# Output bias by one-row matmuls, one VectorE operation for the residual sum, and a placing step moved by a slot

## The reference, cut to what matters

```python
x = x + layernorm(attn0(layernorm(x)))            # phase 0 of the kernel
f = layernorm(x)
for l in range(2):                                # phases 1 and 2
    f = f + _attn(_ln(f, ln1_w[l], ln1_b[l]), ...)   # y @ wo + bo
    h = _ln(f, ln2_w[l], ln2_b[l])
    f = f + moe(h, ...)       # l = 0: two experts per token; l = 1: two per batch
x = x + layernorm(f)
```

## Time and profile before

| | |
|---|---|
| median of 3 runs | 1260.97 us (1259.69 to 1270.06) |
| the profiled execution | 1260.14 us, of it 1258.4 us from the first to the last instruction |
| steps of phases 0 and 1 | to about 620 us |
| expert jobs of phase 1 | about 640 to 775 us |
| steps of phase 2 | about 800 to 1125 us |
| batch experts and end | to 1258 us |

### The profile page before, as it was taken

The page is one execution under the profiler, slowest core; times in us unless marked ns, Lnnn a source line. Parts: engine busy times, 40 slices in busy tenths (PEclk is TensorE's granted clock), DMA queues, the critical chain, the costliest instruction groups (busy, mean ns, idle before and its releaser), DMA issues. The chain is left out here.

```text
span 1258.4 us, 38248 instructions
## 1 busy us (share of the span) xinstructions
PE 1048.2 (83%) x10356; PEld 791.0 (63%) x10451; DVE 974.2 (77%) x2902; ACT 789.2 (63%) x1905; POOL 683.7 (54%) x1018
## 2 busy tenths in 40 slices
PE   1888999999899999998289995487888988959997
PEld 0555666666666666665189995255555655638996
DVE  3678999999998899898647654368899898865665
ACT  1566777777677777776068774266666666745554
POOL 3345565555556778776623333557676676422332
PEclk9999999999999999999589998599999999988999
DMA  5332111111211222111122222233221121100000
GB/s 146 93 99 78 52 46 39 43 51 53 54 52 44 59 66 66 50 57 45 50 63 67 68 71 65 69 113 108 60 66 47 55 65 38 53 1 9 17 21 21
DMA packets 118044, 72.96 MB, mean 58 GB/s; under 512 B 8384, under 2 KB 112960, under 8 KB 117952
## 3 DMA queue, kind: packets, MB, share of 16 engines
q1 hardware_dynamic: 99296, 53.11, 15.2%
q10 hardware_dynamic: 14560, 10.35, 2.9%
q0 software_dynamic: 4096, 8.40, 2.2%
HBM read 21.68 MB, written 11.60 MB: 26 GB/s over the span
## 5 line engine op out<-in xcount | busy, mean ns | idle before, releaser
L608 DVE TENSOR_REDUCE negm<-bank 128x2 f32<-128x512 f32 (+1 forms) x576 | 389.5, 680 | 79.7 <-PE bank L300 55.0
L496 ACT ACTIVATE prob<-bank 128x512 f32<-128x512 f32 x576 | 339.6, 595 | 128.6 <-PE bank L322 90.4
L889 POOL TENSOR_SCALAR_AFFINE_SELECT prob<-prob 128x512 f32<-128x512 f32 x384 | 248.3, 648 | 171.3 <-ACT prob L496 169.7
L341 PE MATMUL bank<-prob,vaug 128*32 128x256 f32 (+1 forms) x3072 | 167.9, 337 | 1.6 <-POOL prob L889 1.3
L1181 POOL COPY w_job<-w_s 128x512 f32 x104 | 67.7, 651 | 164.6 <-PE bank L1150 156.0
L308 PE MATMUL bank<-stack 126*128 126x256 bf16 x768 | 151.7, 279 | 0.0
L327 PE MATMUL bank<-stack 128*128 128x256 bf16 x768 | 150.6, 278 | 0.9 <-ACT prob L496 0.9
L1172 ACT ACTIVATE prob<-bank,b_job 128x128 f32<-128x128 f32 (+1 forms) x416 | 133.4, 398 | 24.7 <-PE bank L1150 11.8
L1161 PE MATMUL bank<-w_job,prob 128*128 128x128 f32 x1088 | 138.9, 276 | 0.1
L1161 PEld LDWEIGHTS bank<-w_job,prob 128*128 128x128 f32 x1088 | 132.2, 192 | 2.1 <-issue 0.5
L341 PEld LDWEIGHTS bank<-prob,vaug 128*32 128x32 f32 x3072 | 81.4, 110 | 77.7 <-issue 45.8
(11 more groups left out here) (180 smaller groups left out, 2073.0 us busy)
## 6 DMA issues: line engine op xcount, KB each, us to landing
stack<-parts SPq DMA_DIRECT2D x288, 128.0 KB
w_s<-e_w ACTq DMA_DIRECT2D x32, 256.0 KB, 3.0
oT<-x_routed SPq DMA_DIRECT2D x72, 64.0 KB, 1.8
y_routed<-oT SPq DMA_DIRECT2D x36, 128.0 KB, 1.9
stack<-mT SPq DMA_DIRECT2D x192, 4.0 KB
out<-x_all SPq DMA_DIRECT2D x16, 128.0 KB, 1.8
b_all<-e_b ACTq DMA_DIRECT2D x2, 512.0 KB, 8.5
x_routed<-hk,x_at POOLq DMA_INDIRECT x64, 2.3
```

Source lines behind the costliest of these rows:

```text
L341: m = nc.tensor.matmul(o, w, (prob0, prob1)[kb][:, g % 2, h], start=kb == 0, stop=kb == 1, skip_group_check=True)
L496: nc.scalar.activation(o, s, ACT.Exp, scale=SCALE).then_inc(exp_done, 1)
L608: nc.vector.tensor_reduce(o, s, AX.X, ALU.max, negate=True).then_inc(max_done, 1)
L889: nc.gpsimd.affine_select(out=t, in_=t, compare_op=ALU.is_ge, fill=0.0, base=0, pattern=[[0, HG], [1, P]], channel_multiplier=-1).then_inc ...
```

## The change

In phases 1 and 2, `pe_o3` leaves the accumulation open and adds, for each of the two token halves, a matmul of one contraction row: a row of ones (1 x 128) as weights, the bias row (1 x 128) as the moving operand. DVE then reads PSUM, adds `f_all` and writes `f_all` in one operation; it raises the semaphore by 2. The bias addition into `att` stays in phase 0. In phase 1 the placing pieces 3 and 4 move from slot 3 to slot 2, piece 5 from the end of slot 3 to its first part.

```diff
@@ pe_o3
                 m = nc.tensor.matmul(post_bank[:, qb * P:(qb + 1) * P], onT[:, i.par, qb * P:(qb + 1) * P],
-                                     wo_s[:, i.phase], start=True, stop=True)
+                                     wo_s[:, i.phase], start=True, stop=i.phase == 0)
+                if i.phase > 0:
+                    m = nc.tensor.matmul(post_bank[:, qb * P:(qb + 1) * P], ones[0:1], bo_s[0:1, i.phase],
+                                         start=False, stop=True)
@@ dve_residual
-            base = NRES * i.v
             dve.wait_ge(o3_ps, i.v + 1)
+            if i.phase > 0:
+                nc.vector.tensor_tensor(pair(f_all, i), post_bank[:, 0:T].rearrange("p (j d) -> p j d", j=2),
+                                        pair(f_all, i), ALU.add).then_inc(res, 2)
+                return
             nc.vector.tensor_tensor(att[:, i.par], post_bank[:, 0:T].rearrange("p (j d) -> p j d", j=2),
                                     bo_s[:, i.phase:i.phase + 1].to_broadcast([P, 2, P]),
                                     ALU.add).then_inc(res, 1)
-            if i.phase > 0:
-                dve.wait_ge(res, base + 1)
-                nc.vector.tensor_tensor(pair(f_all, i), pair(f_all, i), att[:, i.par], ALU.add).then_inc(res, 1)
@@ dve_slot
-                dve_place(first, 3)
+                dve_place(first, 5)
...
+            if k == 2 and placing:
+                dve_place(first, 3)
...
+            if k == 2 and placing:
+                dve_place(first, 4)
...
-            if k == 3 and placing:
-                dve_place(first, 4)
-            if k == 3 and placing:
-                dve_place(first, 5)
```

## The result

The changed kernel takes **1278.41 us** (median of 4 runs, 1276.03 to 1281.16) against 1262.87 (4 runs) for the kernel before in the same comparison: ratio **1.0113, 95% interval 1.0085 to 1.014**. It is slower, outside the predicted range (1246 to 1274). The profiled run took 1281.16 us, its span is 1279.3. It is the longest of its four runs, so the two profiled spans differ by 20.9 us, the medians by 15.5.

The account below looks back on a forecast made before the run. The prediction took the ring POOL, ACT, POOL, SP, DMA, PE as the bound. DVE 0, bias +2.4, placing +2.4, clock -3 gave +1.8 on 1260.14, plus 0.8 to the median: 1262.7, written 1262 us; range 1246 to 1274.

Parts of the forecast that it names:

- The ring: Phases 1 and 2: the chain POOL, ACT, POOL, SP, DMA, PE sets the step's length; L666 is not in it.
- DVE's 0: DVE's residual in phases 1 and 2: about 44 us leaves DVE's queue, 0 us of it on the path.
- the first rival: DVE is the bound after all: PE's waits for `mparts` go, phase 1 steps under 17.5 us, 1243 in all; chance 0.12.
- the 0.81 us foreseen: Sign: L615 or L617 of slot 1 takes 0.8 to 1.0 us in phases 1 and 2, as L615 in phase 0.
- The bias: New bias matmuls on PE ahead of slot 1: +2.4 us in phase 1, bounds 0 and 7.0; phase 2 hidden.
- I take 0.44: Price in us per item of the bias matmuls on PE, from f32 matmuls of 128 x 128; least 0, most 1.2.
- the cover that the sum reckoned with: Phase 1: L554's 0.23 us wait for `rest` hides part of the bias's 0.44 us; 0.15 taken for 16 steps.
- In phase 2 hidden: 0: Phase 2: L554 waits 1.39 us for `rest`, so the bias's 0.44 us is hidden and costs 0.
- The placing: Phase 1, pieces 3 and 4 ahead of `xn`: DVE comes late, +0.2 us in 12 steps, +2.4 us, bounds 0 and 6.
- POOL gains ... I count 0: POOL, which waited 16.6 us for `x_at`, finds it ready; its next select waits for its exponential anyway, so 0.
- The clock: PE's lowered clock in phase 2: five slow steps, up to 1.0 us each; three taken, -3 us.
- The second rival: The bias lies on the ring in full: each item pays 0.44, 14 us, placing 5 us, 1280 in all; chance 0.11.

Follow-up runs that it names:

- e2: The changed kernel with the placing pieces put back where they were, so only one-row bias matmuls and the single DVE addition; 1276.19 us.
- e4: As e2, but the bias product takes all 128 contraction rows (identity by the bias on every partition); 1267.17 us.
- e1: The kernel before with only the placing pieces moved; 1266.93 us.
- e8: The changed kernel with placing piece 5 alone put back to the end of slot 3; 1274.61 us.
- e5: The changed kernel with eight long satisfied waits on DVE ahead of its job loop, moving the loop back to place 1529; 1271.56 us.
- e3: As e2 without the one-row matmuls, so the output bias of phases 1 and 2 is missing from the result; 1281.69 us.
- e6: As e2, but both output products first, then both one-row products; for half the tokens the bias replaces the product; 1270.51 us.
- e10: As e4, with the eight satisfied waits of e5 ahead of DVE's job loop; 1260.69 us, ratio 0.9977.
- e9: The kernel before with the change in phase 2 alone, each 128-row bias product right behind its output product; 1259.62 us, ratio 0.9961.

## Why the prediction was wrong

The sum came to 1262.7 (written as 1262), its upper bound to 1274; the price of the bias products and a stage without a term carried the time past both.

*The ring and DVE's 0*: right. L907 to L322 is 5.61 us in phase 1 and 5.69 in phase 2, as before, and phase 2's step is 18.78 us with L666 and without. So the first rival fell: the step of the ring did not get shorter without L666, and the steps of phase 1 are 17.7 to 19.6 us up to its last two, not under 17.5. L618 took the 0.81 us foreseen. L352 stood 1.82 us behind L907 in phase 1, in phase 2 in every other step 1.25; there L620 was held to the end of L907 and not by the select behind it. L322's wait in phase 2 was 0.27, not 1 us: the one-row matmuls filled that time.

*The bias*: **the step that failed is "I take 0.44"**, taken from 128 x 128 matmuls. The least and most were both priced, 0 and 1.2 us an item, but the bounds of the sum went by 16 x 0.44 = 7.0 and never used the 1.2. The 128-row form costs 0.45 (0.99 - 0.54); one-row products cost 1.12 (1.66 - 0.54), the difference being four changes of the row count. Less the cover that the sum reckoned with, 0.44 - 0.15 = 0.29 a step, that is 16 x 0.83 = 13.3 us (with the cover as the trace before has it, L554's waits for `rest`, 3.8 us in ten of 16 steps, 14.1); e2 measured 13.5, and e4, where the price is the 0.44 foreseen, +2.4, the term of the sum. So the way into the step (ahead of slot 1, through ACT and POOL) was right: in phase 1 no L557 waits for `rest` any more, in the steps of phase 2 it waits 0.13 to 0.29 us in place of 0.9 to 1.4. "In phase 2 hidden: 0" holds for its long steps but not for the last four, 3.6 us longer with one-row products. No run has a matmul of few contraction rows by itself, so the Trainium skill's sentence on 32 of them (TensorE: Matmul & The Clock Gate, Why this matters for your kernels) is neither borne out nor refuted; what cost here was the change between row counts.

*The placing*: the size was right by luck, +2.4 against +2.9 in e1, the mechanism was not. `xn` did go to 1.07 us, but e8 keeps that for nothing. What costs is "POOL gains ... I count 0": a POOL that no longer waits moves its copy and select onto DVE's small operations. On top of the bias it cost more, 1.7 (e5 to e2) to 5.2 us (changed kernel to e2).

*The clock*: -3 predicted; all five of the slow steps are gone instead of three, and they give 6.6 us (100.3 - 93.7) instead of 1.0 each. The last steps take 3.6 back and the first ones give some, so that phase 2 measures -4.6. Its other side was missed: without the matmuls the same DVE saving lowers the clock (e3).

*The job stage*: no term at all, +7.0 us. DVE's program is four instructions shorter ahead of the loop. e5 gives it back with eight waits.

*The second rival* named 1280 and came near in number by luck, not in cause: L557 does follow the exponential in phase 1, but since the bias is 1.12 us long, not because its cover is gone; in phase 2 it still waits for `rest`, and phase 2 gained.

The sum with measured terms: 13.5 + 2.9 and up to 2.3 on top, 7.0, -4.6 and about 0 in the rest, 18.8 to 21.1, against 20.9 between the two spans. The terms come from profiles that differ by some us for the same code, so the agreement says little more than that no large term is missing. The changed kernel, e2, e4, e5, e6, e8 and e10 also have a step in phase 0 that is 1.0 to 1.3 us longer (18.4 in place of 17.3 from item 3 to 4 in the changed kernel, where PE waits 1.33 us at L298 for the DMA of `parts`); the kernels without bias matmuls in phase 1 don't. Its cause is open.

## What to carry to other kernels

A matmul with one contraction row between full ones is not priced by its size: feed the term with all rows if a full operand is at hand, and price the change of row count by itself. Where an unknown price has two bounds, the range must go by the far one. An engine freed of a wait is a new source of collisions: ask which of its instructions now meets whose. And cut every stage of the new profile, those outside the diff too, since a shorter program moves the loops behind it.

## What was unexpected of the hardware

- Each change between 1 and 128 contraction rows cost TensorE 0.15 to 0.17 us (f32, 128 columns).
- At the turn of a loop with the same body DVE issued nothing for 0.85 to 0.91 us with the loop at place 1525 of its program, for 0.53 to 0.73 at 1529, and had no such wait at 1589.
- Of nine steps in phase 1 of e3 with one pause of TensorE of 1.6 to 1.9 us, four had a mean granted clock of 0.91, five 1.00; the steps of the kernel before, with pauses of 0.8 and 0.4 us, had 1.00 throughout. In phase 2 of e9 seven steps running with a pause of 1.5 to 1.6 us and one of 0.4 to 0.65 had 1.00: the pause by itself doesn't settle it.
- In phase 2 the merged addition by itself cost time (277.4 us) and gained with more work on TensorE (266.5 to 269.1), against 271.3 before; that work without the merged addition gave 269.7.
